# The closing feed-forward moved into the second mixer's block, and the wait for constants moved to its first users

## The reference

```
x = _layernorm(x + _L1_attn_ref(x, ...))     # second mixer
x = _layernorm(x + _L1_ffn_ref(x, ...))      # closing feed-forward

# _L1_ffn_ref: W1 (256 x 1024), W2 (1024 x 256) composed from the logits
h = jax.nn.gelu(jnp.einsum('bsd,df->bsf', x, W1))
return jnp.einsum('bsf,fd->bsd', h, W2)
```

## Time and profile before

| | us |
|---|---|
| runs, median of 3 | 4597.69 (4597.64 to 4602.04) |
| profiled execution, its time | 4567.66 |
| its span, first to last instruction | 4565.7 |
| TensorE busy | 3937.4 (86%) |
| VectorE busy | 2462.8 (54%) |
| ScalarE busy | 1990.0 (44%) |
| GpSimd busy | 1089.9 (24%) |

### The profile page before, as it was taken

How to read it: one execution, slowest core, us unless ns; L and a number is a source line. 1 busy time by engine, 2 the same in 40 slices (tenths; PEclk the granted TensorE clock), 3 DMA queues, 4 the chain that set the end, 5 groups by cost and what they waited for, 6 DMA issues and landing times. The chain is left out here.

```text
span 4565.7 us, 72621 instructions
## 1 busy us (share of the span) xinstructions
PE 3937.4 (86%) x23860; PEld 3048.4 (67%) x23860; DVE 2462.8 (54%) x5456; ACT 1990.0 (44%) x4069; POOL 1089.9 (24%) x1689
## 2 busy tenths in 40 slices
PE   5888788598999999993788888888888888769998
PEld 3555555377888888881577666666767677646666
DVE  7888888552222222224577767777777776421111
ACT  5655655111222222212466666666666666432222
POOL 0111111102222222212333433333333332200000
PEclk8888889799999999996799999999999999879999
DMA  1010010245555555552111111111111110011111
GB/s 34 29 42 28 28 42 20 78 133 180 184 184 184 184 184 184 184 169 71 37 38 43 44 37 42 43 42 43 42 43 43 42 43 24 20 51 55 55 55 46
DMA packets 220428, 345.93 MB, mean 76 GB/s; under 512 B 99956, under 2 KB 171380, under 8 KB 201972
## 3 DMA queue, kind: packets, MB, share of 16 engines
q1 hardware_dynamic: 196404, 271.69, 18.7%
q0 software_dynamic: 23760, 71.07, 4.9%
HBM read 275.56 MB, written 67.63 MB: 75 GB/s over the span
## 5 line engine op out<-in xcount | busy, mean ns | idle before, releaser
L525 ACT ACTIVATE moe_rel<-moe_fc 128x512 f32<-128x512 f32 x284 | 169.6, 597 | 799.6 <-PE moe_fc L490 799.6
L490 PE MATMUL moe_fc<-moe_xT,moe_win 128*128 128x256 f32 x2272 | 505.0, 381 | 1.5 <-issue 0.8
L501 PE MATMUL moe_o<-moe_wout,moe_hT 128*128 128x256 f32 x2272 | 502.0, 379 | 0.0
L490 PEld LDWEIGHTS moe_fc<-moe_xT,moe_win 128*128 128x128 f32 x2272 | 433.5, 191 | 61.5 <-issue 2.1
L501 PEld LDWEIGHTS moe_o<-moe_wout,moe_hT 128*128 128x128 f32 x2272 | 426.3, 190 | 55.1
L549 DVE TENSOR_TENSOR moe_hT<-moe_rel 128x512 f32<-128x512 f32 x284 | 196.7, 693 | 362.0 <-ACT moe_rel L525 362.0
L1777 DVE SCALAR_TENSOR_TENSOR gdr_y<-gdr_bank,gdr_cw,gdr_y 128x511 f32<-128x511 f32 (+2 forms) x384 | 287.5, 749 | 81.2 <-ACT gdr_y L2045 61.5
L2252 PE MATMUL gdr_bank<-gdr_hT,gdr_wqkv 128*128 128x512 f32 x512 | 260.4, 633 | 41.3 <-ACT gdr_qk L2060 24.7
L558 DVE COPY moe_osb<-moe_o 128x512 f32<-128x512 f32 x71 | 49.1, 692 | 424.9 <-PE moe_o L501 424.9
L723 DVE TENSOR_TENSOR ffn_z<-ffn_o,ffn_xres 128x512 f32<-128x512 f32 x32 | 20.6, 686 | 381.2 <-PE ffn_o L690 381.2
L690 PE MATMUL ffn_o<-ffn_wout,ffn_hT 128*128 128x256 f32 x1024 | 225.2, 381 | 0.0
(11 more groups left out here) (391 smaller groups left out, 8398.3 us busy)
## 6 DMA issues: line engine op xcount, KB each, us to landing
moe_win<-in_moe_w SPq DMA_DIRECT2D x71, 1024.0 KB, 8.0
moe_wout<-in_moe_w SPq DMA_DIRECT2D x71, 1024.0 KB, 5.2
slots_out<-moe_osb POOLq DMA_DIRECT2D x71, 256.0 KB, 7.5
ffn_xin<-mixed_rows SPq DMA_DIRECT2D x17, 512.0 KB, 3.8
gla_xp<-in_xT_rows SPq DMA_DIRECT2D x16, 512.0 KB, 4.7
gla_xres<-in_x_rows SPq DMA_DIRECT2D x16, 512.0 KB, 3.9
token_rows<-gla_x POOLq DMA_DIRECT2D x16, 512.0 KB, 3.4
rt_W<-in_fc_b SPq DMA_DIRECT2D x32, 256.0 KB, 3.3
```

The source lines that it names most:

```text
L490: ins = nc.tensor.matmul(fc_ps[j][:, m % 2, :], win[u][:, c, m * P:(m + 1) * P], xT[:, c, :], start=(c == 0), stop=(c == DT - 1))
L501: ins = nc.tensor.matmul(o_ps[u][:, t, :], hT[u][:, k, t * P:(t + 1) * P], wout[u][:, k, :], start=(k == 0), stop=(k == FT - 1))
L525: nc.scalar.activation(rel[:, j, :, :], fc_ps[j][:], ACT.Relu).then_inc(relu_done, 1)
```

## The change

mlp and its block are gone. A function closing takes the mixer's tiles and PSUM banks that are dead at its end, and returns seven pieces, which are put into the mixer's own engine functions: one behind the end of each engine's program, and two, load and load_next, into SP's periods 16 and 17. win is loaded over wqkv, wout over vn, xin over fz, hT lies in sq, nAT and T, xT in the mixer's hT, osb in xn, xres in x2, z in kb; fc uses banks 6, 7, 4, 5, turn banks 1, 2, and o banks 0, 3. The identity, mhalf and hold are the mixer's. Rows are loaded one block further ahead, so the copy behind the last row is of 1024 rows. The waits for ready and aprep move from the head of period -1 to slot 11 (TensorE) and slot 13 (VectorE) of it, and on ScalarE to the head of period 0.

```diff
@@ closing @@
+    def load(sp):
+        sp.wait_ge(x3_stored, 16)
+        sp.dma_start(xin[:], rows(0)).then_inc(x_in, 16)
+        sp.dma_start(win[:], w_in.rearrange("(t p) f -> p t f", p=P)).then_inc(win_in, 16)
+        sp.dma_start(wout, w_out.rearrange("(t p) d -> p t d", p=P)).then_inc(wout_in, 16)
+        sp.wait_ge(x3_stored, 32)
+        sp.dma_start(x_rows[NTOK:NTOK + 2 * BLK, :], x_rows[0:2 * BLK, :]).then_inc(tail_in, 16)
+
+    def load_next(sp):
+        sp.wait_ge(x_turned, 1)
+        sp.dma_start(xin[:], rows(1)).then_inc(x_in, 16)
+
+    def sync(sp):
+        sp.wait_ge(x3_stored, B * 16)
+        sp.wait_ge(tail_in, 16)
+        with sp.Fori(0, N) as n:
+            here, after = rows(n), rows(n + 2)
+            sp.wait_ge(o_ready, n * 2 + 2)
+            sp.dma_start(xres[:], here).then_inc(res_in, 16)
+            sp.wait_ge(x_turned, n + 2)
+            sp.dma_start(xin[:], after).then_inc(x_in, 16)
+        sp.wait_ge(x_in, 16 * (N + 2))
...
+    def tensor(pe):
...
+        pe.nop().then_inc(xT_ready, 1)
+        pe.nop().then_inc(o_done, 1)
+        pe.nop().then_inc(h_ready, 1)
+        turn(0)
+        pe.wait_ge(win_in, 16)
+        pe.wait_ge(wout_in, 16)
+        with pe.Fori(0, N) as n:
+            pe.wait_ge(xT_ready, n * 2 + 3)
...
+    def scalar(act):
+        act.wait_ge(yb, B * 2)
+        act.nop().then_inc(o_ready, 2)
+        act.wait_ge(x_turned, 1)
+        for c in range(DT):
+            nc.scalar.copy(xT[:, c, :], tp_ps[c][:]).then_inc(xT_ready, 1)
+        with act.Fori(0, N) as n:
...
@@ SP, period @@
+                    if isinstance(b, int) and b == B:
+                        sp.wait_ge(s["pj"], B * NP_)
+                        sp.wait_ge(s["ab_ps"], B)
+                        sp.wait_ge(s["vb"], B * 2)
+                        sp.wait_ge(s["hT_ps"], B)
+                        fc_load(sp)
+                    if isinstance(b, int) and b == B + 1:
+                        fc_load_next(sp)
                     if end:
                         dst = by_row(x3_rows, b - 2)
@@ SP, end @@
                 loop(sp, period)
-                sp.wait_ge(x3_stored, B * 16)
+                fc_sync(sp)
@@ VectorE, period @@
-                    if isinstance(b, int) and b == -1:
-                        dve.wait_ge(ready, 1)
...
                         if slot == 13 and front:
+                            if not later(b, -1):
+                                dve.wait_ge(ready, 1)
                             decay(b + 1, w)
@@ ScalarE, period @@
-                    if isinstance(b, int) and b == -1:
+                    if isinstance(b, int) and b == 0:
                         act.wait_ge(ready, 1)
@@ TensorE, period @@
-                    if isinstance(b, int) and b == -1:
-                        pe.wait_ge(ready, 1)
-                        pe.wait_ge(aprep, 3)
...
                         if front and slot == 11:
+                            if not later(b, -1):
+                                pe.wait_ge(ready, 1)
+                                pe.wait_ge(aprep, 3)
                             reach(b + 1)
```

More of the change, by code:

```diff
@@ L1419, in delta_rule @@
 def delta_rule(nc, x1_rows, slots_out, get_at, weight, ln1_g, ln1_b, rms_w, wq, wk, wv, conv_q, conv_k, conv_v, wa, dt_bias, a_log, wb, wg,
-               o_norm, wo, ln2_g, ln2_b, w2, b2, x2_rows, hT_rows, blocks_out, blocks_in, x3_rows):
+               o_norm, wo, ln2_g, ln2_b, w2, b2, x2_rows, hT_rows, blocks_out, blocks_in, x3_wide, fc1, fc2, out_rows):
     with ExitStack() as ctx:
@@ L1495, in delta_rule @@
         id0, id1, cst, ready = sem("id0"), sem("id1"), sem("cst"), sem("ready")
+        x3_rows = x3_wide[0:NTOK, :]
+        fc_load, fc_load_next, fc_sync, fc_gpsimd, fc_tensor, fc_scalar, fc_vector = closing(
+            nc, sem, ident, wqkv, vn[:].rearrange("p t h n -> p (t h n)").rearrange("p (t d) -> p t d", d=D), fz, hT,
+            [sq[:, m, :] for m in range(TT)] + [m_[:, i, :, :].rearrange("p h n -> p (h n)") for m_ in (nAT, T) for i in range(2)],
+            xn, x2, kb[:].rearrange("p t h n -> p t (h n)"), stats[0], agg[0], var[0], rstd[0], mhalf[:, 0:TT], hold,
+            [bank[n] for n in (*FRONT, *CHUNK)], [bank[n] for n in YZ], [bank[n] for n in (UT, SIDE)],
+            x3_wide, fc1, fc2, out_rows, s["yb"], x3_stored)
         def waiter(eng, b):
@@ L1707, in _ @@
                 loop(pool, period)
+                fc_gpsimd(pool)
             @block.vector
@@ L2018, in _ @@
                 loop(dve, period)
+                fc_vector(dve)
             @block.scalar
@@ L2229, in _ @@
                 loop(act, period)
+                fc_scalar(act)
             @block.tensor
@@ L2502, in _ @@
                 loop(pe, period)
+                fc_tensor(pe)
 INPUTS = dict(
@@ L2520, in build_program @@
     scratch = lambda name, rows, cols: nc.dram_tensor(name, (rows, cols), F32).ap()
-    x1_rows, x3_wide = scratch("token_rows", NTOK, D), scratch("mixed_rows", NTOK + BLK, D)
-    x3_rows = x3_wide[0:NTOK, :]
+    x1_rows, x3_wide = scratch("token_rows", NTOK, D), scratch("mixed_rows", NTOK + 2 * BLK, D)
     logits = scratch("router_logits", NTOK, EXPERTS)
@@ L2542, in build_program @@
                    ("ln1_g", "ln1_b", "rms_in_w", "Wq", "Wk", "Wv", "conv_q_w", "conv_k_w", "conv_v_w", "Wa", "dt_bias",
-                    "A_log", "Wb", "Wg", "o_norm_w", "Wo", "ln2_g", "ln2_b", "W2", "b2")], x2_rows, hT_rows, blocks_out, blocks_in, x3_rows)
-    mlp(nc, x3_wide, w1, w2, out_rows, 1, NTOK // BLK, True)
+                    "A_log", "Wb", "Wg", "o_norm_w", "Wo", "ln2_g", "ln2_b", "W2", "b2")], x2_rows, hT_rows, blocks_out, blocks_in, x3_wide, w1, w2, out_rows)
 def kernel(**inputs):
```

221 lines of the change are left out of this document (62 added, 159 removed).

## The result

The changed kernel takes 4569.03 us (median of 4 runs, 4564.02 to 4570.64), the kernel before 4599.86 in the same comparison. The ratio on record is 0.9924, 95% interval 0.9907 to 0.9941, so 27 to 43 us faster; the two medians by themselves are 30.8 us apart, a quotient of 0.9933. The forecast was 4569.3.

The account below looks back on a forecast made before the run. TensorE was taken as busy nearly everywhere but for two waits, at the second mixer's start and its border to the feed-forward. 16.3 + 11.6 + 0.5 = 28.4 us off the median 4597.69 gave 4569.3 us, range 4564 to 4575, widened to 4560 to 4580.

Parts of the forecast that it names:

- Part 1, the border: Mixer's end into feed-forward: with one block, the first fc matmul moves from 4094.19 to 4077.88, gaining 16.3 us.
- a lost cover: Feed-forward loads, covered by batch 15's work: without cover, each us of lateness past 4077.9 would cost one.
- The clock: fc(0) at the border: 15.62 us against fc(1)'s 13.90; bounds of gain 0 and 1.7 us, 0.5 taken.
- the 3.55 us row: Gap at 2189.22 with slow transposes after it; nearest evidence for the clock after fc(0)'s wait, read as nearer no gain.
- Part 2, the constants: Mixer's start, period -1: without the wait for GpSimd's last constant, projection 0 starts at 2103.80, gaining 11.6 us.
- (a) to (c): Period -1, things not moving up: constants, spare 41 us; batch 1's gathered rows, spare 7; GpSimd's power, free for 10.
- The sum: Whole kernel: 16.3 + 11.6 + 0.5 = 28.4 us gained.
- The subtraction from the median: Whole kernel: gains are waits of fixed length, so 28.4 us comes off the median 4597.69, giving 4569.3 us.
- The moved wait: Rival, mixer's start: gather rows or GpSimd's power hold VectorE as long as constants held TensorE; 4580.9 us, chance 0.08.
- the loads weren't late: Rival, border: SP reaches feed-forward loads only behind the last store, leaving 4.2 of 16.3 us; 4581.9 us, chance 0.05.
- the loop didn't slow: Rival, feed-forward loop: late xin loads make TensorE wait once a block; at 3 us each 4617 us, chance 0.03.
- stall at its turn: Rival, feed-forward loop: each of 15 loop turns waits for an instruction fetch, 24 us back; 4593.3 us, chance 0.02.

Follow-up runs that it names:

- the block alone: Changed kernel with the waits for constants back at the head of period -1, feed-forward still in the mixer's block: 0.9964 to the kernel before.
- the kernel with the copies first: Changed kernel with ScalarE's two copies of the transposed rows ahead of the mixer's last Gelu: 0.9927 to the kernel before, median 4568.16 us.
- the kernels with the waits alone: Kernel before with only the waits for constants moved, feed-forward in its own block: 0.9956, then 0.9970; with constants also made early 0.9960.
- the job with the halves: Unedited changed kernel run again beside one kernel with only the waits moved and one with only the common block: 0.9933 to the kernel before.
- the kernels with fc in the gaps: Changed kernel with block 0's fc between pieces of batch 15's output: 0.9908; second also with ScalarE's bank release and block 1 copies before last Gelu: 0.9910.

## Why the prediction was right

**Part 1, the border (16.3 us).** Measured 16.2 in the profile; the runs of the block alone gave 16.6, and 15.3 by their medians. The chain behind dense was as worked out, to 0.1 us: Gelu, copies, fc(0). One term is missing from the sum: the 1.9 us that the program with one block takes longer behind its last store. The price put on a lost cover was too low. The prediction left 4.2 of the 16.3 us in that case; with the loads behind the last store nothing was left, fc(0) came 16.1 us later than in the changed kernel. Part of it is that the loop now waits for wout as well, which the old kernel asked for only ahead of o(0): ScalarE's copies were over at 4111.99, and fc(0) started at 4114.91. That each us of lateness costs one was not tested by degrees.

**The clock (0.5 us).** This term was 0. fc(0) took 15.63 us after the change, 15.62 before, and 16.85 in the block alone, although dense had run at the full level there. The premise that dense would be at the full clock held in that kernel and not in the changed one (3.78 us in both its profiles). The Trainium skill (TensorE: Matmul & The Clock Gate, What's actually happening: the default state is throttled, activity releases it) came out nearer than my reading of the 3.55 us row. The 1.7 us were there to be had, as the kernel with the copies first shows, with the wait cut to 1.3 us.

**Part 2, the constants (11.6 us).** The wait itself: 11.67 measured. None of (a) to (c) became late. Period -1 gained 13.5 us in the kernels with the waits alone, for which the clock is no explanation; the runs of the waits alone say 14 and 20, with 11.6 inside the second interval and outside the first. So this term may be too small by some us, and where they come from is open.

**The sum (28.4 us).** Measured 35 (27 to 43) and 31 (24 to 37) by the ratios, 30.8 and 27.5 by the medians. The forecast of 4569.3 met the median of 4569.03, and that is luck to a good part. It subtracted from a median of 4597.69, and the 69 later runs of the kernel before gave 4602.3 to 4605.2 by job, 5 to 7 us more. In the job with the halves the changed kernel had a median of 4576.78. And inside the sum a gain from the clock that did not come, the cost at the end that was not seen, and a period that gained more than its wait partly cancel.

**The subtraction from the median** was right and needed: the gains are waits, the profiled execution was an unusual one. My reason for the range (pauses of 16 batches fall differently on the clock) fits what the runs show, and the range was too narrow: the stretch between the two places took 1958 to 1994 us over twelve executions of which I had one, the shortest; the other eleven took 1978 to 1994. A block of the feed-forward took 28.57 us before (4153.06 - 4124.49) and 28.58 after (4154.44 - 4125.86), not 28.7: the sum of 14.84 and 13.90 counts the overlap of fc and turn twice.

**The rivals.** The moved wait wasn't given back, the loads weren't late, the loop didn't slow and had no stall at its turn: TensorE is busy 340.00 of 340 us after as before. So the stall behind a taken branch, of which the Trainium skill speaks (Runtime: NRT & Kernel Launch, Instruction fetch mechanics), did not show at the turn of this loop.

## What to carry to other kernels

At a border between stages, ask of the first matmul behind it what it truly needs. Here it needed rows and weights that had been ready for long, and waited for a store, a barrier and loads that belonged to the end of the other stage. Joining the programs gives nothing by itself (and cost 1.9 us at the end here); issuing the loads ahead of the last store does, and once they are there, the gaps of the old stage's drain can take the new stage's first work (7 to 11 us more here by the ratios). A wait for constants belongs at their first user; but a kernel whose single profile is 30 us off its median has to be judged by pieces of the timeline and by repeated runs, not by spans.

## What the runs showed of the hardware

One program's time varies here by more than 0.5%, and goes with the granted clock of TensorE. Of 29 runs of the kernel before in one job, the 9 with a mean granted clock of 0.923 or more took 4595.8 us on average, the 10 with 0.919 or less 4606.9; the execution profiled first had 0.927 and took 4567.66. Single periods of the mixer took 111 to 125 us for the same instructions.

A wait of TensorE of 3.1 to 3.7 us was followed by matmuls at the low level (fc(0) in 15.6 to 16.9 us), one of 1.3 us was not (13.99). A short wait is no guarantee, though: in the kernels with fc in the gaps, waits of 1.8 and 1.3 us around turn(0) were followed by 16 records in 9.15 and 9.34 us in place of 7.03. So in a stage of short waits, a gain or a loss of a microsecond or two at one place can be given back or doubled by the clock behind it, and only many runs show it.
